# Attention over 16 batches with a routed feed-forward: DMA issues, early work of batch 1 and window counts of batch 0 rearranged

## The reference

```python
B, N, D, M, H = 16, 256, 128, 1601, 16
# attention: queries from the normalised rows, keys and values from ctx
qh = einsum('bnd,hde->bhne', layernorm(x), Wq)
kh = einsum('bmd,hde->bhme', ctx, Wk)
vh = einsum('bmd,hde->bhme', ctx, Wv)
att = softmax(einsum('bhne,bhme->bhnm', qh, kh) * 0.125)
x = x + tanh(g_xattn) * (concat_heads(att @ vh) @ Wo.T)
# feed-forward: 8 experts, the best 2 for each row
probs = softmax(layernorm(x) @ router_w.T)
cw = the two largest, divided by their sum
out = sum over e of cw[:, e] * (new_gelu(x2 @ w1[e].T + b1[e]) @ w2[e].T + b2[e])
x = x + tanh(g_ffn) * out
```

## Time and profile before

| | us |
|---|---|
| median of 3 runs | 1363.93 |
| lowest and highest | 1360.14, 1364.64 |
| the profiled execution | 1353.72 |
| its span, first to last instruction | 1351.9 |
| first scores of unit 0 | 47.84 |
| last scores of unit 51 | 127.8 |

### The profile page before, as it was taken

How to read it: one execution, slowest core, us unless ns; L and a number is a source line. 1 busy time by engine, 2 the same in 40 slices (tenths; PEclk the granted TensorE clock), 3 DMA queues, 4 the chain that set the end, 5 groups by cost and what they waited for, 6 DMA issues and landing times.

```text
span 1351.9 us, 37790 instructions
## 1 busy us (share of the span) xinstructions
PE 1294.0 (96%) x13888; PEld 626.4 (46%) x13888; DVE 1164.9 (86%) x2268; ACT 1097.9 (81%) x2190; POOL 543.6 (40%) x1208
## 2 busy tenths in 40 slices
PE   5899999999999999999999999999999999999992
PEld 2334444444444444444444444444444444388882
DVE  7788999999999999999999999999999999456444
ACT  2378898988888889898989888898989888965661
POOL 3032526262626253535344444535262603135441
PEclk7699999999999999999999999999999999999997
DMA  3222121212121212122222222121211110187886
GB/s 115 64 84 73 45 69 49 71 48 77 43 82 37 68 50 63 55 63 62 57 66 59 64 60 66 53 67 51 71 47 43 49 48 10 43 260 212 238 242 226
DMA packets 61076, 109.84 MB, mean 81 GB/s; under 512 B 13052, under 2 KB 36476, under 8 KB 60748
## 3 DMA queue, kind: packets, MB, share of 16 engines
q1 hardware_dynamic: 54340, 95.48, 24.3%
q0 software_dynamic: 4320, 8.99, 2.0%
q10 hardware_dynamic: 2232, 2.96, 0.6%
HBM read 49.96 MB, written 13.71 MB: 47 GB/s over the span
## 4 chain that ended last, share of the span: by engine, by line
PE 77%; DVE 17%; issue 3%; DMA 1%; SPq 1%; ACT 1%; POOL 0%; POOLq 0%; DVEq 0%
PE pv L813 28%; PE st L765 14%; DVE mx L1553 14%; PE mxp L787 13%; PE st L1048 5%; PE mxp L1058 4%; PE st L871 4%; PE st L885 3%; PE st L843 1%; PE st L897 1%; PE st L855 1%; PE st L920 1%; PE st L930 1%; DVE x_sb L1748 1%; PE mxp L1023 1%
## 5 line engine op out<-in xcount | busy, mean ns | idle before, releaser
L1553 DVE TENSOR_REDUCE mx<-mxp 128x2 f32<-128x804 f32 x1024 | 985.8, 988 | 70.8 <-PE mxp L787 61.0
L1087 ACT ACTIVATE arena<-st 128x512 f32<-128x512 f32 (+1 forms) x1664 | 891.7, 595 | 85.8 <-PE st L765 79.4
L813 PE MATMUL pv<-arena 128*32 128x256 f32 x6656 | 534.2, 393 | 0.4 <-ACT pv_sb L1094 0.4
L787 PE MATMUL mxp<-kpack,qpack 48*128 48x402 bf16 x2048 | 464.6, 343 | 24.4 <-DVE mx L1553 15.3
L765 PE MATMUL st<-qpack,kpack 51*128 51x256 bf16 (+1 forms) x3328 | 457.9, 273 | 0.2
L765 PEld LDWEIGHTS st<-qpack,kpack 51*128 51x128 bf16 (+1 forms) x3328 | 200.6, 96 | 208.5 <-ACT arena L1087 115.6
L787 PEld LDWEIGHTS mxp<-kpack,qpack 48*128 48x128 bf16 x2048 | 146.0, 93 | 164.1 <-DVE mx L1553 80.8
L813 PEld LDWEIGHTS pv<-arena 128*32 128x32 f32 x6656 | 131.5, 108 | 176.8 <-ACT arena L1087 90.2
L1225 ACT ACTIVATE arena<-st,bias 128x256 f32<-128x256 f32 (+1 forms) x172 | 74.9, 437 | 49.2 <-PE st L1048 46.2
L652 POOL CAST mxs<-nmx 128x8 bf16<-128x8 f32 x64 | 12.2, 191 | 254.5 <-DVE nmx L1561 254.3
L685 POOL DMA_INDIRECT rows<-xrow,pos x64 | 66.0, 1031 | 95.2 <-DVE pos L1410 80.0
(11 more groups left out here) (193 smaller groups left out, 948.7 us busy)
## 6 DMA issues: line engine op xcount, KB each, us to landing
kpack<-ksp SPq DMA_DIRECT2D x762, 50.0 KB
arena<-in_w12T SPq DMA_DIRECT2D x43, 512.0 KB, 4.3
arena<-in_ctxT SPq DMA_DIRECT2D x15, 800.5 KB, 4.4
qpack<-qsp SPq DMA_DIRECT2D x187, 32.0 KB
xblk<-rows SPq DMA_DIRECT2D x28, 132.0 KB, 3.5
rows<-in_pads SPq DMA_DIRECT2D x8, 264.0 KB, 4.4
qpack<-mxT SPq DMA_DIRECT2D x128, 3.0 KB
arena<-results SPq DMA_DIRECT2D x8, 256.0 KB, 7.0
```

What stands on the lines that cost most here:

```text
L787: eng.matmul(mxp[pair % MX_BUFS][:, rg, 0:WIN], qpack[rows, b % 2, g * JJ + jj, t * P:(t + 1) * P], kpack[rows, b % 2, g * JJ + jj, WSTART ...
L813: ins = eng.matmul(pv[32 * j:32 * j + 32, 0:N], vaug[0:n, b % 2, kt, at:at + 32], pt[0:n, (2 * u + rg) % PT_BUFS, jj * N:(jj + 1) * N], st ...
L1087: eng.activation(pt[0:n, c % PT_BUFS, :], ring[bank_of["S", u, p]][0:n, :], ACT.Exp, scale=SCALE).then_inc(s_exp, 1)
L1553: eng.tensor_reduce(mx[:, tj, w, :], mxp[windows_done % MX_BUFS][:, :, 0:WIN], AX.X, ALU.max).then_inc(s_red, 1)
```

## The change

It has four parts.

1. ACT issues 18 of the 36 DMAs for the keys of groups 1 to 3 of batch 0 and one of the two for group 0's maxima. SP keeps the other half. SP's load of batch 1's ctx, its ones rows for batch 1 and the load of batch 2's rows move to later places.
2. The rows and queries of batch 1 are made ahead of the first window, into the upper half of `mxp1` and into `pv`.
3. The values of batch 1 are made in batch 0 at r = 25 to 28, as those of later batches are in theirs.
4. Batch 0 gets its own window strings, `FIRST_WINDOWS_AT`. 22 windows stand ahead of the first unit instead of 23. The batch makes 70 instead of 71, all of them at the end of units, and the head start `LEAD` of all later batches is 28 instead of 30.

```diff
-X1_AHEAD, Q1_AHEAD, V1_AHEAD = 1, 2, 8
-LEAD, SHORT = 30, 7
+FIRST, LEAD = 22, 28
 WINDOWS_AT = ("1011011110111111111111101001101110011111110111100111",
               "1101111020000000000001101211100011100000011000120000")
+FIRST_WINDOWS_AT = ("0000000000000000000000000000000000000000000000000000",
+                    "2111211212221111211111111211222211111211122111211112")
...
 def issued(u, p):
     b, r = divmod(u, UNITS)
-    return LEAD + b * PER_BATCH + ISSUED[2 * r + p] - max(0, SHORT - u // 3)
+    if b == 0:
+        return FIRST + FIRST_ISSUED[2 * r + p]
+    return LEAD + b * PER_BATCH + ISSUED[2 * r + p]
...
-        k0p, x0p, q0p = [*st, mxp[0][:, 0, :]], mxp[0][:, 1, :], mxp[1][:, 0, :]
+        k0p = [*st, mxp[0][:, 0, :]]
+        x_first, q_first = [mxp[0][:, 1, :], mxp[1][:, 1, :]], [mxp[1][:, 0, :], pv]
...
+        def place_half(eng, G, rg):
+            b, g = divmod(G, NG)
+            r, rows = rg * RSTEP + MAXROW, KINDS * JJ
+            eng.dma_start(qpack[r:r + KINDS, b % 2, g * JJ:(g + 1) * JJ, :],
+                          mxT[rg * rows:(rg + 1) * rows, :]).then_inc(s_mxd[G % 2], 16)
...
             first_packs(eng, 0)
             pack_query_rows(eng, 0, PARTS - 1, 1)
-            eng.dma_start(ctx_sb[:, 1, :], ctxT[1]).then_inc(s_ctx[1], 16)
-            pack_keys(0, 1)
+            def other_keys(g):
+                for part in range(PARTS):
+                    pack_key_rows(eng, 0, g, part, 0)
+            other_keys(1)
             eng.wait_ge(s_kone, 1)
             ones_rows(0)
-            pack_keys(0, 2)
-            place_maxima(0)
-            pack_keys(0, 3)
+            other_keys(2)
+            eng.dma_start(ctx_sb[:, 1, :], ctxT[1]).then_inc(s_ctx[1], 16)
+            other_keys(3)
+            eng.wait_ge(s_mxT, 1)
+            place_half(eng, 0, 0)
             pack_queries(1)
...
-            ones_rows(1)
-            load_rows(2)
...
                     if r == 9:
+                        ones_rows(1)
+                        load_rows(2)
                         load_context(0)
                     elif r == 14:
                         pack_keys(1, 0)
+                        pack_keys(1, 1, range(PARTS // 2))
                     elif r == 23:
-                        pack_keys(1, 1)
+                        pack_keys(1, 1, range(PARTS // 2, PARTS))
...
             for c in range(NV - 1):
                 values(0, c)
+            turn_rows("X", 1)
+            queries(1)
             for n in range(issued(0, 0)):
+                if n == 1:
+                    eng.wait_ge(s_xnT, 2)
                 maximum(*divmod(n, NMX))
                 if n == 0:
                     values(0, NV - 1)
-                elif n == X1_AHEAD:
-                    turn_rows("X", 1)
-                elif n == Q1_AHEAD:
-                    queries(1)
-                elif V1_AHEAD <= n < V1_AHEAD + VCH[0][1]:
-                    values(1, 0, [n - V1_AHEAD])
                 elif n == NMX + 1:
                     turn_maxima(0)
-                elif n > NMX + 1 and n - NMX - 1 < NV:
-                    values(1, n - NMX - 1)
...
-                    elif b > 0 and r in V_AT:
+                    elif r in V_AT:
                         values(b + 1, V_AT[r])
...
             first_packs(eng, 1)
-            for c in range(NV):
+            copy_rows(1)
+            for c in range(NV - 1):
                 copy_values(0, c)
+            first_queries(1)
+            copy_values(0, NV - 1)
             eng.wait_ge(s_id, 16)
             eng.activation(id_bf[:, :], id_sb[:, :], ACT.Copy).then_inc(s_idb, 1)
-            copy_rows(1)
-            first_queries(1)
-            copy_values(1, 0)
+            for g in range(1, NG):
+                for part in range(PARTS):
+                    pack_key_rows(eng, 0, g, part, 1)
             copy_maxima(0)
-            for c in range(1, NV):
-                copy_values(1, c)
+            eng.wait_ge(s_mxT, 1)
+            place_half(eng, 0, 1)
```

More of the change, by code:

```diff
@@ L107 @@
 ROWS_AT, LAST_ROWS_AT = {1: 40, 2: 42, 3: 44}, {9: 0, 10: 1, 11: 2, 12: 3}
-LEAD, SHORT = 30, 7
+FIRST, LEAD = 22, 28
 WINDOWS_AT = ("1011011110111111111111101001101110011111110111100111",
               "1101111020000000000001101211100011100000011000120000")
+FIRST_WINDOWS_AT = ("0000000000000000000000000000000000000000000000000000",
+                    "2111211212221111211111211222211111211122111211121112")
 PER_BATCH = NG * NMX
-ISSUED = [sum(int(WINDOWS_AT[q][r]) for r in range(UNITS) for q in range(2) if 2 * r + q < c)
-          for c in range(2 * UNITS)]
+ISSUED, FIRST_ISSUED = [[sum(int(at[q][r]) for r in range(UNITS) for q in range(2) if 2 * r + q < c)
+                         for c in range(2 * UNITS)] for at in (WINDOWS_AT, FIRST_WINDOWS_AT)]
 def key_rows(kt):
@@ L145, in prepared @@
         return "K", b + 1, keys_at(b)[r]
-    if 0 < b < B - 1 and r in V_AT:
+    if b + 1 < B and r in V_AT:
         return "V", b + 1, V_AT[r]
@@ L451, in place_maxima @@
             def place_maxima(G):
-                b, g = divmod(G, NG)
                 eng.wait_ge(s_mxT, G + 1)
-                rows = KINDS * JJ
                 for rg in range(RG):
-                    r = rg * RSTEP + MAXROW
-                    eng.dma_start(qpack[r:r + KINDS, b % 2, g * JJ:(g + 1) * JJ, :],
-                                  mxT[rg * rows:(rg + 1) * rows, :]).then_inc(s_mxd[G % 2], 16)
+                    place_half(eng, G, rg)
             def load_rows(b):
@@ L832, in turn_rows @@
             def turn_rows(kind, b):
-                if (kind, b) == ("X", 0):
-                    dst = x0p
+                if kind == "X" and b < 2:
+                    dst = x_first[b]
                 else:
@@ L872, in keys, with values @@
                            start=True, stop=True).then_inc(s_kp, 1)
-            def values(b, c, some=None):
+            def values(b, c):
                 i = bank_of["V", b, c]
                 t0, tn = VCH[c]
-                some = range(tn) if some is None else some
-                if 0 in some:
-                    eng.wait_ge(*freed[i])
-                    if b == 1 and c == 0:
-                        eng.wait_ge(s_ctx[1], 16)
-                for t in some:
+                eng.wait_ge(*freed[i])
+                for t in range(tn):
                     n = key_rows(t0 + t)
@@ L1096, in copy_rows @@
             def copy_rows(b):
-                src = ring[bank_of["X", b]] if b > 0 else x0p
+                src = ring[bank_of["X", b]] if b > 1 else x_first[b]
                 eng.wait_ge(s_xp, b + 1)
@@ L1103, in first_queries @@
                 if b > 0:
[L1104 removed]
+                    src = ring[bank_of["Q", b]] if b > 1 else q_first[b]
                     eng.wait_ge(s_qd[(b - 1) % 2], 16 * PACKS * ((b - 1) // 2 + 1))
@@ L1616, in _ @@
                             [ksp[:, n, k0:k0 + kn] for n in range(KINDS)], (s_khi, c + 1), s_k3)
-            split_first(q0p[:, 0:N], qf[:, :], [qsp[:, n, :] for n in range(KINDS)], (s_qhi, 1), s_q3)
+            split_first(q_first[0][:, 0:N], qf[:, :], [qsp[:, n, :] for n in range(KINDS)], (s_qhi, 1), s_q3)
             for n in range(5):
```

13 lines of the change are left out of this document (4 added, 9 removed).

## The result

The changed kernel takes 1376.87 us (median of four runs, 1374.73 to 1378.06); the kernel before, timed beside it, takes 1363.34 (four runs, 1360.14 to 1364.64). The ratio is 1.0108 with a 95% interval of 1.0093 to 1.0123: **slower by 1.1%, or 13.5 us**. The forecast of 1356.9 and its range up to 1362.5 are both missed, with the wrong sign.

What follows compares the result with a forecast made beforehand. PE bounds the middle, so gains lie in the opening, set by DVE's windows, and batch 0. Batch 0 ends 7.4 us earlier, less 0.4 for windows made up later: 1363.9 - 7.0 = 1356.9 us, range 1350.0 to 1362.5.

Steps and rivals of the forecast that it cites:

- the step on later batches: Later batches: a head start of 28 moves each maximum by two windows and costs 0, at most 1 us in all.
- The prediction's own sign for this: Middle batches: the prediction is wrong if PE's idle there exceeds the 0.5% of before.
- the moves on SP: SP's ones, batch 2's rows and half a group's keys: they go into SP's idle time and cost 0.
- The opening: Stretch up to the first scores: unit 0 starts at 43.7 instead of 47.8, 4.1 us earlier.
- Landing: Opening: arrival of group 0's placed maxima after their issue, taken as 1.7 us, bounded by 0 and 3.3.
- ACT's issues: Opening: 18 key issues on ACT at 0.66 us each, 11.9 us, ending at 37.0, before the copy needs ACT.
- The rival on them: Opening: ACT's issues hold up the first maxima; at 0.99 us each ACT is 2.1 us late, gain 4.9; chance 0.07.
- the half clock at the first scores: Start of batch 0: first units run at half clock for 6 us, a loss of 3.0 us.
- the stall at r = 8: Batch 0, unit 8: PE stands 1.6 us for group 1's maxima, between 0.5 and 2.7.
- six in ten: Batch 0: odds that the clock falls after the stall at r = 8, put in at 1.2 us.
- The clock did not oscillate on: Batch 0 rival: half clock for 17.0 us again instead of 8.4, gain 2.7 us, 1361.2; chance 0.2.
- the others in batch 0: Further rivals: it goes better, gain 11.1, chance 0.2; values come back in full, gain 3.7, chance 0.08.

Runs made afterwards that it cites:

- e1: Changed kernel with the old head start of 30 and 24 windows ahead of unit 0: 1362.22 us, ratio 1.0010 to the kernel before.
- e2: Kernel before with a head start of 28 instead of 30, still 23 windows ahead of unit 0: 1372.93 us, ratio 1.0081.
- e9 to e11: Kernel of e7 with head starts of 29, 31 and 32 instead of 30: 1360.62, 1352.80 and 1348.47 us.
- e3: Changed kernel with SP's six key issues moved from r = 14 to r = 23, behind group 2's maxima: 1371.48 us, ratio 1.0069 to the kernel before.
- e4: Changed kernel with the edits of e1 and e3 together: 1355.24 us, ratio 0.9949 to the kernel before.
- e7: Kernel of e4 with SP placing both halves of group 0's maxima and batch 0's last double window at unit 49 instead of 51: 1346.76 us, ratio 0.9956.
- e5: Kernel of e3 with head transpositions and DVE's divisions at r = 4 and 44 instead of 2 and 42: 1366.06 us, ratio 1.0096 to the kernel before.
- e12: Kernel of e7 with batch 1's values made ahead of the first scores again: 1348.85 us, ratio 0.9962 to the kernel before.
- e8: Kernel before with only the sharing of the keys: ACT issues half of groups 1 to 3 of batch 0: 1352.95 us, ratio 1.0005.

## Why the prediction was wrong, step by step

**The main failure is the step on later batches.** It said that two windows later change nothing and costed it at 0, at most 1 us in all. It asked a single question of the changed head start: is each maximum still in time for the engine that turns it? That was answered correctly; no middle batch waits for `mxs`. It did not ask what else moves with the head start. The windows stand at fixed units, so with two windows fewer in hand the last window of a group is one of another unit, and `nmx` moves with it. DVE is at 93.74 of 100 us in the earlier trace rows and feeds PE two banks at a time, so a step in the wrong unit shows on PE. The price is 0.97 us a batch, 12.6 over the thirteen. e1 took it away and e2 put it into the old kernel; e9 to e11 show that the position counts and not the margin. That it works through `nmx` is argued from where that step stands. The prediction's own sign for this fired: PE's idle share from 200 to 300 us is 0.99% instead of 0.50%. The prediction counted DVE's `nmx` in batch 0's sum and did not look for its place in the others.

**The second failure is the sentence that the moves on SP go into its idle time and cost 0.** SP has idle time in sum, but it issues in order. By the earlier trace rows a key issue takes 0.61 us, so six more at r = 14 put 3.7 us ahead of whatever comes next on SP (12.24 / 18 = 0.68 each in the trace, 4.1 us), and next come maxima for which PE waits. The prediction named what is queued behind PE's wait at r = 8 and did not do the same for SP. The price was a wait of 4.4 us and half clock for 3.4 us; in e1 it was 4.0 and 10.2. In e3, without it, batch 0 took 77.3 us. The forecast for it was 77.5, and that they agree is partly luck: e3 had 12.2 us at half clock where 8.4 were forecast, 1.9 us more of loss, and the waits for DVE and the work were shorter by about as much.

**The opening missed by 2.4 us.** 46.1 instead of 43.7 is the sum of two mis-sized terms. Landing was taken at 1.7 us, between 0 and 3.3; it was 3.6, 0.3 above the upper bound. The row taken for it was a burst of queries. The 3.3 of the kernel before was no landing time either, since PE was busy until then, its last window held by DVE:

```profile
47.66 0.34 PE L787 MATMUL mxp<-kpack,qpack 48*128 48x402 bf16 x2 [0.48 <-DVE mx L1553]
```

And ACT's issues took 0.96 each on average, not 0.66; the median was taken where a few long issues set the sum. ACT was 1.0 us late for the copy, and its issues ran to 41.26, beyond the 41 that the prediction named as a sign of being wrong. The rival on them had this price (0.99) and said 2.1 us late. Its last step has a wrong sum: at 2.0 us each, 20 us late is 1377, not 1370. DVE's part was 0.6 better than forecast. In the range, half of the named bounds give a gain of 2.5 to 9.3, not 3.3 to 9.5; the stated range holds both.

**What held.** The order of the opening, the half clock at the first scores (6 forecast, 6.1), the stall at r = 8 (1.6 forecast, 1.6), one more fall of the clock, and DVE's windows (2.0 us forecast, 1.4). The fall did not come at r = 8, where PE stood for 1.6 us: the clock stayed at 1.00 there and fell behind the 4.4. In e3 it did come at r = 8, behind the same 1.6 us, so the prediction's six in ten for it was a fair choice. At r = 25 the changed kernel was 9.4 us ahead of the kernel before. With the two failures undone, in e4, batch 1 starts at 120.73 (forecast 121.2) and the gain is 5.5 us (forecast 7.0). The agreement at 120.73 is a sum of two misses: the first scores come 2.8 us later than forecast and batch 0 is 3.2 us shorter, also because e4 has two windows more in hand and so no stall at r = 8. Of the 6.5 us by which its batch 0 is shorter than before, some 4.8 are the clock's (7.4 us at half instead of 17.0, halved: an estimate), and 4.8 less waiting for DVE is set against 3.5 for the values. The lost part is mostly in the unit where batch 1 begins: a double window at the end of batch 0 meets two in the next unit, 2.14 us instead of 1.25. The forecast did not look at the border; e7 gets back 0.9 of it with batch 0's end counted in.

**The rivals.** None of them was this. The clock did not oscillate on: 9.5 us at half, not 17.0. The prediction had weighed a rule of the Trainium skill (TensorE: Matmul & The Clock Gate, A second HAM failure mode: psum-queue depth-cycling) by which it would. The trace of e4 disagrees: the clock is at 1.00 from 53.8 through all the later batches, with the same two banks. But the rival's amount is not out of reach: e1, with the changed opening, had 18.1 us at half clock in batch 0, 10.2 of them behind one wait of 4.0. ACT's issues cost half of what their rival said and did not decide. The rival for slower lay in the opening and the others in batch 0; the mechanism that decided lay in the stage that was said to be untouched.

**What stays open.** Which of DVE's neighbours makes `nmx` dear in a given unit is not settled. The form that e5 tested, the division behind it, fell, and no kernel moved `nmx` alone. Nor is it known what the landing at the opening consists of. PE stood for it in nine kernels, and from the end of the issue to the scores they took 2.8 to 4.0 us. At r = 23 the same transfer took 2.0 (changed kernel) and 1.7 (e1, e12), and in e8, placed 1.0 us behind the last key issue, at most 2.5. That fits keys' packets still under way ahead of the maxima, which no run tried without keys. Why the clock fell behind 1.6 us in one kernel and not in the other, and stayed low for 3.4 us in one and 10.2 in another, is open too.
